# Scales folded into weights, a batch norm taken in two parts, and a new order of work in a four-layer kernel

## The reference

```python
x = x + L0(_gn(x))   # softmax attention: q, k, v of 128x128, scores 256x256, Wo
x = x + L1(_gn(x))   # batchnorm -> sign -> 3x3 grouped conv with sign weights -> batchnorm -> + res -> PReLU
x = x + L2(_gn(x))   # depthwise 3x3 -> bn -> relu -> prune(4.0) -> pointwise 128x128 -> bn -> relu -> prune(0.001)
x = x + L3(_gn(x))   # linear attention: softmax(k) over positions, context = k v^T per head, out = context q, w_out
# _batchnorm: mean and variance over images and positions, one pair for each channel
# _prune(x, t): amax of each image and channel; zeros where amax < t, otherwise x
```

## Time and profile before

| what | value |
|---|---|
| time, median of 3 runs | 70.32 us (70.3 to 70.65) |
| the profiled execution | 70.66 us, of which the span from first to last instruction is 68.9 us |
| busy share of the span | PE 89%, DVE 72%, ACT 51%, POOL 43% |
| DMA | idle between the loads at the start and the stores at the end |

### The profile page before, as it was taken

The page is one execution under the profiler, slowest core; times in us unless marked ns, Lnnn a source line. Parts: engine busy times, 40 slices in busy tenths (PEclk is TensorE's granted clock), DMA queues, the critical chain, the costliest instruction groups (busy, mean ns, idle before and its releaser), DMA issues.

```text
span 68.9 us, 1300 instructions
## 1 busy us (share of the span) xinstructions
PE 61.5 (89%) x376; PEld 51.3 (74%) x376; DVE 49.3 (72%) x196; ACT 35.2 (51%) x103; POOL 29.4 (43%) x81
## 2 busy tenths in 40 slices
PE   3999989999996999859999699999994999999940
PEld 2777888899895878548888488888873688898710
DVE  3946897675939876898359999998955878843450
ACT  5111407577686950292005757375363976877600
POOL 6807142878999806417030048062983304300000
PEclk9999999999999999999999999999999999999998
DMA  0985000000000000000000000000000000020033
GB/s 0 237 247 214 0 0 0 0 0 0 5 10 0 5 0 0 0 0 0 10 0 0 5 0 0 0 0 0 0 5 0 0 0 0 10 76 0 0 114 114
DMA packets 1431, 1.81 MB, mean 26 GB/s; under 512 B 144, under 2 KB 1168, under 8 KB 1424
## 3 DMA queue, kind: packets, MB, share of 16 engines
q1 hardware_dynamic: 1424, 1.73, 8.2%
HBM read 1.20 MB, written 0.52 MB: 25 GB/s over the span
## 4 chain that ended last, share of the span: by engine, by line
PE 53%; POOL 19%; DVE 16%; issue 7%; ACT 1%; POOLq 0%; DVEq 0%; ACTq 0%
PE bank L1204 12%; PE bank L1321 6%; POOL conv_blocks L356 4%; PE bank L1349 4%; PE bank L1374 3%; POOL dw_dev_rstd_bias L409 3%; PE bank L1391 3%; PE bank L1222 3%; PE bank L1431 3%; PE bank L1384 3%; PE bank L1411 3%; PE bank L1255 2%; DVE gn_var_eps L719 2%; POOL dw_limit L412 2%; PE bank L1278 2%
## 5 line engine op out<-in xcount | busy, mean ns | idle before, releaser
L329 POOL TENSOR_TENSOR gn_rstd<-gn_var_eps,minus_half 128x1 f32<-128x1 f32 x12 | 6.8, 569 | 12.6 <-DVE gn_var_eps L719 12.3
L1349 PE MATMUL bank<-x,dw_diag 128*128 128x256 f32 x48 | 11.3, 385 | 0.0
L1204 PE MATMUL bank<-warm 128*128 128x256 bf16 x60 | 9.3, 321 | 1.2 <-POOL warm L311 1.2
L1349 PEld LDWEIGHTS bank<-x,dw_diag 128*128 128x128 f32 x48 | 8.8, 189 | 1.1
L1204 PEld LDWEIGHTS bank<-warm 128*128 128x128 bf16 x60 | 6.8, 115 | 2.7 <-POOL warm L311 1.1
L1321 PE MATMUL bank<-signs,conv_blocks 128*128 128x256 bf16 x36 | 4.3, 276 | 1.0 <-ACT signs L521 1.0
L725 DVE TENSOR_SCALAR t<-x,gn_group,gn_rstd 128x256 f32<-128x256 f32 x8 | 3.3, 417 | 2.2 <-POOL gn_rstd L329 2.0
L409 POOL TENSOR_TENSOR dw_dev_rstd_bias<-gn_var_eps,root_powers 128x2 f32<-128x2 f32 x4 | 3.2, 789 | 4.0 <-DVE gn_var_eps L719 3.9
L1321 PEld LDWEIGHTS bank<-signs,conv_blocks 128*128 128x128 bf16 x36 | 3.4, 97 | 1.8 <-issue 1.2
L531 ACT ACTIVATE h_neg<-h,bn_shift 128x256 f32<-128x256 f32 x4 | 1.9, 498 | 5.5 <-DVE bn_shift L871 5.5
L1335 PE MATMUL bank<-valid,dw_diag 128*128 128x256 f32 x18 | 4.5, 388 | 0.0
(11 more groups left out here) (154 smaller groups left out, 158.5 us busy)
## 6 DMA issues: line engine op xcount, KB each, us to landing
out<-x SPq DMA_DIRECT2D x4, 128.0 KB, 1.7
late_params<-in_late SPq DMA_DIRECT2D x1, 404.5 KB, 4.7
early_params<-in_early SPq DMA_DIRECT2D x1, 258.0 KB, 2.8
...
```

Of the source, the lines that this page charges most:

```text
L329: return nc.gpsimd.tensor_tensor(out_ap, in_ap, minus_half[:, 0:n], ALU.pow)
L1204: nc.tensor.matmul(bank[:, 0:N], warm[:, 0:C], warm[:, :], start=True, stop=True)
L1349: ins = nc.tensor.matmul(dw_ps[b], dw_diag[:, tap, :], xs[2][:, b, dy:dy + H, dx:dx + W], start=(tap == 0), stop=(tap == PE_TAPS - 1))
```

## The change

The change does these things:

1. `fold_bias` reads the bias columns from the loaded parameters with a step of zero; `bias_broadcast` and its tile are gone from POOL. It stands before the first projection in PE's list, its copy `v_bias_out` second in ACT's, and `keep_warm` there has 13 and 3 calls, not 14 and 6.
2. POOL does `x_bias(1)` before `l2_constants`, and `conv_weights` after `x_bias(3)`.
3. The last image's part of the first batch norm: `x1_out(3)` sums each half as it writes it, ACT squares each half (`x1_square`), and two matmuls add the halves' group sums. The part of images 0 to 2 is worked out by itself (`bn1_rest_*`), the last by `bn1_last_*`.
4. The last two `valid_taps` stand behind the conv; `keep_warm` there has 28 calls, not 36.
5. The pointwise weights are multiplied by the batch norm's scale: transposed on PE, scaled on ACT, transposed back, copied on ACT (`pw_forward`, `pw_scaled_out`, `pw_back`, `pwT_out`).
6. With the scale in the weights the bank holds everything but the shift. relu, shift and prune become one maximum: `prune2_limit` makes a floor for each channel, -shift, or 1 - shift where the image is pruned; `x3_out` writes max(bank, floor) + x2 straight from the bank. x3 is then too high by minus the floor: `x3_sum_out`, `x3_group_mean`, the bias of `square_sum3` and `out_bias_out` put that right. `relu2` is gone.
7. Depthwise is issued in two halves with the group sums between or behind them, and the lists of DVE, ACT, POOL and PE for layers 2 and 3 are in another order.

```diff
...
-            def bias_broadcast():
-
-                pool.wait_ge(early_in, 16)
-                for i, name in enumerate(("bv", "bo")):
-                    ins = nc.gpsimd.tensor_scalar(bias_rows[:, i, :], ones[:, :], ep[:, EC[name]], 0.0,
-                                                  ALU.mult, ALU.add)
-                ins.then_inc(pool_consts, 1)
-
...
+                step(nc.gpsimd.tensor_scalar(l2_limit2[:, :], l2_shift[:, 1:2], -1.0, PW_THRESH,
+                                             ALU.mult, ALU.add))
...
+            def out_bias_out(b):
+
+                pool.wait_ge(pw_floor_ready, b + 1)
+                nc.gpsimd.tensor_tensor(out_bias[:, b:b + 1], lp[:, LC["b_out"]], pw_floor[:, b:b + 1],
+                                        ALU.subtract).then_inc(out_bias_ready, 1)
...
             x_bias(0)
             gn_root(0, 3)
+            x_bias(1)
             l2_constants()
-            conv_weights()
-            x_bias(1)
             x_bias(2)
             x_bias(3)
+            conv_weights()
...
             dw_mean_out(2)
             dw_limits(2)
+            gn_root(3, 0)
+            out_bias_out(0)
             dw_mean_out(3)
             dw_limits(3)
-            gn_root(3, 0)
             gn_root(3, 1)
+            out_bias_out(1)
             gn_root(3, 2)
+            out_bias_out(2)
             gn_root(3, 3)
+            out_bias_out(3)
...
+            def pw_scaled_out():
+
+                act.wait_ge(pw_setup_mm, 1)
+                act.wait_ge(l2_consts, 1)
+                nc.scalar.activation(pw_scaled[:, :], pw_setup_ps, ACT.Copy,
+                                     scale=l2_scale[:, 1:2]).then_inc(pw_setup_out, 1)
+
+            def pwT_out():
+
+                act.wait_ge(pw_setup_mm, 2)
+                nc.scalar.activation(pwT[:, :], pw_setup_ps, ACT.Copy).then_inc(pw_setup_out, 1)
...
+            def x1_square(par):
+
+                act.wait_ge(x1_ready, 2 * B - 1 + par)
+                side = slice(par * HALF, (par + 1) * HALF)
+                nc.scalar.activation(squares[:, 0, 0, side], xs[1][:, B - 1, side], ACT.Square,
+                                     accum_out=x1_sums[:, par, 1:2]).then_inc(x1_sq_ready, 1)
...
+            def square_sum3(b):
+
+                act.wait_ge(x3_ready, b + 1)
+                act.wait_ge(pw_floor_ready, b + 1)
+                nc.scalar.activation(squares[:, 1, b, :], xs[3][:, b, :], ACT.Square,
+                                     bias=pw_floor[:, b:b + 1], scale=-1.0,
+                                     accum_out=mv[:, 3, b, 2:3]).then_inc(stats_ready[3], 1)
...
-            def relu2(b):
-                act.wait_ge(pw_mm, b + 1)
-                nc.scalar.activation(y2[:, b, :], pw_ps, ACT.Relu, bias=l2_shift[:, 1:2],
-                                     scale=l2_scale[:, 1:2]).then_inc(y2_ready, 1)
...
+            def x1_totals():
+
+                dve.wait_ge(x1_ready, 2 * B)
+                dve.wait_ge(x1_sq_ready, 2)
+                step(nc.vector.tensor_tensor(x1_total[:, :], x1_sums[:, 0, :], x1_sums[:, 1, :], ALU.add),
+                     "x1_total")
...
+            def x1_variance():
+                settle("x1_mean")
+                step(nc.vector.scalar_tensor_tensor(
+                    out=x1_var[:, :], in0=x1_mean[:, 0:1], scalar=x1_mean[:, 0:1], in1=x1_mean[:, 1:2],
+                    op0=ALU.mult, op1=ALU.subtract, reverse1=True), "x1_var")
...
+            def bn1_e2_out():
+
+                settle("bn1_last_sq")
+                settle("bn1_last_inv")
+                settle("bn1_rest_eps")
+                step(nc.vector.scalar_tensor_tensor(
+                    out=bn1_e2[:, :], in0=bn1_sq[:, B - 1:B], scalar=bn1_inv[:, B - 1:B],
+                    in1=bn1_rest[:, 1:2], op0=ALU.mult, op1=ALU.add), "bn1_e2")
...
             def prune2_max(b):
-                dve.wait_ge(y2_ready, b + 1)
-                step(nc.vector.tensor_reduce(amax[:, b, 1:2], y2[:, b, :], X_AXIS, ALU.max),
+                dve.wait_ge(pw_mm, b + 1)
+                step(nc.vector.tensor_reduce(amax[:, b, 1:2], pw_ps, X_AXIS, ALU.max),
                      "amax", 1, b)
 
-            def prune2_keep(b):
+            def prune2_limit(b):
+
                 settle("amax", 1, b)
-                step(nc.vector.tensor_scalar(keep[:, b:b + 1], amax[:, b, 1:2], PW_THRESH, None,
-                                             ALU.is_ge), "keep", b)
+                dve.wait_ge(l2_consts, 1)
+                nc.vector.scalar_tensor_tensor(
+                    out=pw_floor[:, b:b + 1], in0=amax[:, b, 1:2], scalar=l2_limit2[:, :],
+                    in1=l2_shift[:, 1:2], op0=ALU.is_lt, op1=ALU.subtract).then_inc(pw_floor_ready, 1)
 
             def x3_out(b):
 
-                settle("keep", b)
+                dve.wait_ge(pw_floor_ready, b + 1)
                 nc.vector.scalar_tensor_tensor(
-                    out=square(xs[3][:, b, :]), in0=square(y2[:, b, :]), scalar=keep[:, b:b + 1],
-                    in1=x2_inside[:, b], op0=ALU.mult, op1=ALU.add,
-                    accum_out=mv[:, 3, b, 0:1]).then_inc(x3_ready, 1)
-
-
+                    out=square(xs[3][:, b, :]), in0=square(pw_ps), scalar=pw_floor[:, b:b + 1],
+                    in1=x2_inside[:, b], op0=ALU.max, op1=ALU.add,
+                    accum_out=x3_sum[:, b:b + 1]).then_inc(x3_ready, 1)
+
+            def x3_sum_out(b):
+
+                dve.wait_ge(x3_ready, b + 1)
+                nc.vector.scalar_tensor_tensor(
+                    out=mv[:, 3, b, 0:1], in0=pw_floor[:, b:b + 1], scalar=-float(N),
+                    in1=x3_sum[:, b:b + 1], op0=ALU.mult, op1=ALU.add).then_inc(x3_sum_ready, 1)
+
+            def x3_group_mean(b):
+
+                dve.wait_ge(group_read[3], b + 1)
+                step(nc.vector.tensor_tensor(x3_mean[:, b:b + 1], gs[:, 3, b, 0:1], pw_floor[:, b:b + 1],
+                                             ALU.add), "x3_mean", b)
 
             def norm3(b):
-                normalise(3, b, t3[:, b, :], b + 1)
+
+                dve.wait_ge(rstd_ready[3], b + 1)
+                settle("x3_mean", b)
+                nc.vector.tensor_scalar(t3[:, b, :], xs[3][:, b, :], x3_mean[:, b:b + 1],
+                                        rstd[:, 3, b:b + 1],
+                                        ALU.subtract, ALU.mult).then_inc(t_ready[3], 1)
...
+                dve.wait_ge(out_bias_ready, b + 1)
                 nc.vector.scalar_tensor_tensor(out=xs[4][:, b, :], in0=y_ps[b],
-                                               scalar=lp[:, LC["b_out"]], in1=xs[3][:, b, :],
+                                               scalar=out_bias[:, b:b + 1], in1=xs[3][:, b, :],
...
+            gamma_doubled()
             x1_out(3)
             group_out(1, 2)
-            x1_stats(3)
...
             group_out(3, 0)
             dw_merge(2)
-            prune2_max(1)
+            prune2_limit(1)
             group_var(3, 0)
+            x3_group_mean(0)
             border_rows(3)
             prune1_keep(2)
-            prune2_keep(1)
+            group_var(2, 3)
+            x3_out(1)
             border_cols(3)
-            x3_out(1)
             norm3(0)
+            x3_sum_out(1)
             dw_merge(3)
+            prune2_max(2)
             prune1_keep(3)
+            group_out(3, 1)
+            prune2_limit(2)
+            group_var(3, 1)
...
+                if layer == 3:
+                    pe.wait_ge(x3_sum_ready, b + 1)
...
-                pe.wait_ge(pool_consts, 2)
-                nc.tensor.matmul(bias_ps, bias_rows[:, 0, :], ep[:, EC["woT"]],
+                pe.wait_ge(pool_consts, 1)
+                nc.tensor.matmul(bias_ps, ep[:, EC["bv"]].to_broadcast([C, C]), ep[:, EC["woT"]],
                                  start=True, stop=False)
-                nc.tensor.matmul(bias_ps, bias_rows[:, 1, :], ident[:, :],
+                nc.tensor.matmul(bias_ps, ep[:, EC["bo"]].to_broadcast([C, C]), ident[:, :],
                                  start=False, stop=True).then_inc(setup_mm, 1)
+
+            def last_x1_means():
+
+                pe.wait_ge(sum_masks, 1)
+                take_bank7(group_read[1], B)
+                for par in range(2):
+                    pe.wait_ge(x1_ready, 2 * B - 1 + par)
+                    pe.wait_ge(x1_sq_ready, par + 1)
+                    ins = nc.tensor.matmul(gn_ps[:, 0:2], group_sum[:, :], x1_sums[:, par, :],
+                                           start=(par == 0), stop=(par == 1))
+                ins.then_inc(group_ready[1], 1)
...
+            def depthwise(b, first, last):
+
+                if first == 0:
+                    pe.wait_ge(x2_ready, b + 1)
+                    if b == 1:
+                        pe.wait_ge(valid_ready, 1)
+                    elif b >= 2:
+                        pe.wait_ge(kept_ready, b - 1)
+                for tap in range(first, last):
                     dy, dx = tap // 3, tap % 3
...
```

(35 more changed lines are left out.)

325 lines of the change are left out of this document (191 added, 134 removed).

## The result

The changed kernel takes 67.51 us (median of 4 runs, 67.37 to 67.84) against 70.32: a ratio of 0.960, 95% interval 0.955 to 0.964. The forecast was 67.3, range 66.2 to 68.9. The profiled execution took 67.55 us.

What follows compares the result with a forecast made beforehand. It took a chain mostly on PE, with stretches on POOL and DVE, as the bound. 0.7 + 0.6 - 0.05 + 1.6 + 0.9 = 3.75, less 0.75, net 3.0: 70.32 becomes 67.3 us, range 66.2 to 68.9.

Steps and rivals of the forecast that it cites:

- Start and x_bias: Layer 0 to last x1_out: 0.44 from fold_bias moved ahead, 0.46 from early x_bias; 0.7 taken, between 0.4 and 0.9.
- First batch norm: Last x1_out to first sign: 4.6 us by DVE's new list instead of 5.34; 0.6 taken, between 0.2 and 1.0.
- Second batch norm and depthwise start: Conv to first depthwise matmul: three taps first start depthwise 0.5 earlier, less 0.05 at the second batch norm: 0.45.
- Second prune: Layer 2: relu2, 0.565 us and a handoff per image, goes from ACT; DVE gets about 0.25 more per image, 1.0 altogether.
- DVE pays the full length: Rival: each added DVE instruction costs all it lasts, 1.7 us instead of 1.0; total 68.0; chance 0.07.
- The step into layer 3: Earlier root of image 0 on POOL starts layer 3 on PE at 51.2, not 52.79: 1.6, including 0.5 from depthwise.
- Layer 3: First projection to last x4_out: 11.2 us of work, waits fall from 2.3 to about 1.4; gain 0.9, between 0 and 1.3.
- layer 3 keeps its length: Rival: PE's new order trades one wait for another, 13.5 us stay; total 68.2; chance 0.16.
- The deduction of 0.75 for DVE and POOL: Taken off the summed gain because DVE and POOL get in each other's way; two collisions of 0.39, bounds 0 and 1.5.
- Bank 6 as a loop: Slower rival: pointwise waits for the previous image's x3_out on DVE; total 71.0, chance 0.04, or 70.4 within noise, 0.03.
- the front that gives nothing: Rival: port conflicts in layer 0 and the weights' copy holding back the signs cancel the early gains; 68.6; chance 0.10.
- The signs that I named: Trace checks: x1_out to sign 4.6 to 4.8, first sign 28.0, no norm3(0) wait of 1.3, projection about 50, then 12.6.

Runs made afterwards that it cites:

- bn1_taps: Kernel before, with the first batch norm in two parts and taps 7 and 8 with their copy moved behind the conv: 69.60 us against 70.33.
- relu2_back: Changed kernel with relu2 on ACT and the second prune as before, without the floor and its small mending instructions; scaled weights and new order kept: 68.58 us.
- root_var_back: Changed kernel with image 0's layer 3 root and out_bias behind image 3's limits on POOL, and group_var(2,3) ahead of group_out(3,0) on DVE: 67.78 us.
- square_first: Changed kernel with square_sum3(2) ahead of q3_out(0) in ACT's list: 66.99 us.

## Why the prediction was right, and where by luck

**Start and x_bias: 0.7 forecast, 1.07 in the two profiles, 0.76 from the first scores on.** The sum is right, its parts are not. Alone, `fold_bias` gave 0.70 where I had 0.44, and x_bias 0.21 where I had 0.46. Adding 0.44 and 0.46 as two separate gains was wrong in kind: after the fold, x_bias has 0.03 left to give (6.74 to 6.71). What the working left out is that POOL's `x_bias(0)` waited 1.40 us for the copy of the folded bias, so that the fold moved POOL's list too, by 0.77.

**First batch norm: 0.6 forecast, 0.77 there, 0.73 by the run with both parts.** My count of 4.6 us along DVE's list was right (4.57). The copy of the turned weights costs nothing there, as I had hoped, but without slack: it starts at 27.26, and the signs follow `bn_shift` after 0.30 us (27.17 to 27.47), as they do in `bn1_taps`, which has no such copy (27.93 to 28.23). What the step left out is that moving the two taps was a condition of it: I priced them at nothing for the conv, and they are worth the difference of 5.03 to 4.57.

**Second batch norm and depthwise start: 0.45 forecast, 0.53.** Right. The 0.5 for the three taps ahead of the group sum was too small as a single edit: taken back alone, it costs 0.86.

**Second prune.** Right in kind: removing relu2 was worth 1.07. The maximum over the bank lasts 0.42 us, as that over y2 in `relu2_back`. My 0.25 us for each image on DVE was a little too much: the spacings make it about 0.20 (0.07 each for `x3_sum_out` and `x3_group_mean`, 0.13 for the limit where the keep took 0.07). So "DVE pays the full length" fell: eight more of 0.15 us would have taken 1.2 us of the list, and at 0.07 each they take 0.56. The Trainium skill, page "VectorE: DVE Perf Modes", section "The DRAIN you can't avoid", has the rule that I took for this rival, that the next instruction does not start until the pipe is empty; it adds that one that is not held starts earlier, which I left out. The trace agrees with the addition, as far as rows of 0.15 us here follow each other after 0.07.

**The step into layer 3: 1.1 (beyond the 0.5) forecast, 0.71.** `norm3(0)` came where I had it: 48.60 is 50.44 in the old time base (the conv starts 1.84 us earlier) against 50.5. But the root's place, which I gave as the reason, is not what the step gained: `root_var_back` puts the wait for the root back (0.62 us at `norm3(0)`), and the first projection comes 0.09 later by it. The first projection came at 51.55 against 51.2, because I walked DVE's list and didn't sum PE's: eight half depthwise pieces, three pointwise and five group sums are 13.04 us on the chain without a gap, where my walk left 12.7.

**Layer 3: 0.9 forecast, 0.22.** This is the step that failed. I had 11.2 us of matmuls and 1.4 us of waits; the waits are 2.1. The rival "layer 3 keeps its length" was nearer to the stage than my case, though its total of 68.2 was farther. The missing part has a place: `q3_out(0)`, which waits for PE, stood on ACT ahead of squares that were ready, 0.40 us of it shown by `square_first`. The other 0.3 was not tried, so its cause stays open; in its chain a q projection takes 0.58 where a 128x256 pair alone takes 0.43, and it waits for ACT's copy of v out of the same bank.

**The deduction of 0.75 for DVE and POOL.** It made the total right for a reason that no run bears out. The 0.60 us of the kernel before is the longest of its sixteen `gn_var_eps`, whose mean is 245 ns; the changed kernel has

```profile
L757 DVE SCALAR_TENSOR_TENSOR gn_var_eps<-gn_group 128x1 f32<-128x1 f32 x16 | 3.4, 214 | 0.2
```

and none above 0.22 us; there `x_bias(0)` runs at 9.94 and beside none of them. One larger instruction lasts longer in its place:

```profile
10.23 0.58 DVE L763 TENSOR_SCALAR t<-x,gn_group,gn_rstd 128x256 f32<-128x256 f32 x1
```

where such a `t` lasts 0.41. So the collisions became fewer, not more. Counted from the first scores, the three terms at the front were 0.31 too small in sum and the two at the back 1.07 too large; the walk promised 0.76 more than came, and the deduction happened to be 0.75. That is luck.

**Bank 6 as a loop, and the front that gives nothing.** Neither came. The only idle time ahead of a pointwise is 0.27 us at the last one (51.26), put down to relu1 of the same image; `x3_out(2)` ends at about the same time, so that there is no slack there, as the walk had it. The front gave 1.84 to the first sign, 1.53 from the first scores on.

**The signs that I named.** From the last `x1_out` to the first sign 4.57 (4.6 to 4.8 forecast), the first sign at 27.47 (28.0), the first projection at 49.71 (about 50), no wait of 1.3 ahead of `norm3(0)`. The one that failed is the length of layer 3: 13.30, not 12.6.
